# Cross stage of a decoder kernel: rounds of scores placed singly, context in thirds, the FiLM halves of two different tiles in one pass

## The chip, the cores and the metric

The kernel runs on one core of a Trainium2 chip. The metric is the device time of one execution in microseconds (us). The kernel before takes 5044.64 us (median of 3 runs, 5043.18 to 5045.29). PE is the matrix engine (TensorE), ACT the ScalarE, DVE the VectorE, POOL the GpSimd engine, SP the engine that issues most of the DMA transfers. Each engine works through its own queue of instructions in the order in which they are written; semaphores hold an instruction back until another engine has come far enough.

## The reference, cut to what matters

The whole program is one decoder layer on 4 sequences of 1024 tokens, width 512: a causal linear attention, a cross attention with a convolution along the sequence, and a quantised feed-forward network. The change lies in the cross stage, which computes:

```python
scores = einsum('bthd,bghd->bhtg', Q, K) / sqrt(DH)          # 4 heads of 32, 2048 context rows
scores = where(vision_mask, scores, -inf)
topv, topi = top_k(scores, 32)
attn = zeros.at[..., topi].set(softmax(topv))                  # 32 weights a row, zeros elsewhere
attn_mean = attn.mean(axis=1)                                  # mean over the 4 heads
c_t = einsum('btg,bgd->btd', attn_mean, x_vision @ Wv)
scale_in, shift_in = split(c_t @ W_film_in + b_film_in)        # "FiLM", inner half
x = layernorm(x_text) * (1 + gate * scale_in) + gate * shift_in
y = s4d(x, ...)                                                # a long convolution along the sequence
scale_out, shift_out = split(c_t @ W_film_out + b_film_out)    # FiLM, outer half
y = y * (1 + gate * scale_out) + gate * shift_out
```

## The kernel before, in words

The 4096 tokens are 32 tiles of 128 (`TILES`); tile t has 4 heads, and head h of tile t is job j = 4t + h (`NH2` = 4). For every job the cross stage does this:

- **Scores** (PE, `scores`, L1161). For a pair p of heads there are four rounds c, one for each 512 columns of the 2048 context rows. In a round each of the two heads has one product of 32 rows of the array (L1169) and a product of one row that adds the mask (L1170). The two heads use the two banks of the PSUM tile `c_p_s`, and the next round waits until ACT has copied the bank out (`copy_s`, L1334).
- **Scan** (DVE, L1490 to L1498). The 32 largest scores of each row are found by four MAX8 over 2048 columns with three MATCH_REPLACE8 between them. `z_done` tells that the scan of a job is over. Before the third MAX8 of job j stands `invert(j - 1)`, the reciprocal L1483, which needs the sum that ACT forms for job j-1.
- **below** (ACT, L1340 to L1346): after `z_done` the threshold, the amount by which each score lies below it, and the sum of the exponentials. **cut** (POOL, L1555) subtracts that amount times a large factor; **weigh** (ACT, L1352) takes the exponential of the whole row; **diagonal** (ACT, L1358) makes the diagonal matrix of 1/sum.
- **attn** (PE, L1179): 16 products of 128x128 that transpose and scale the weights and add them over the heads in `c_p_a`. After the fourth head ACT copies the sum (`copy_a`, L1363).
- **context** (PE, L1231): 48 products of 128x128, the weights times the context values, into `c_p_m`; ACT copies it (`copy_u`, L1368).
- **film** (PE, L1249 and L1250): two halves, each of 6 products of 128x512 and 2 for the bias. Part 0 is the inner half (copied by `copy_fi`, used by POOL's `modulate`), part 1 the outer half (`copy_fo`, stored by `store_mod`).
- **queries** (PE, L1154 and L1158): the tile's x turned, copied by ACT, and multiplied by Wq.

Into the same queues go the pieces of the convolution, one job of 64 channels in a tile of time. `spectra` (PE, L1199: 16 products of 128x64) is copied by `copy_f` (ACT, L1388); POOL then does `transform` (L827 to L850), `convolved` (L1601 to L864) and `finished` (L872 and on), and `slot` (PE, L1219: 16 products of 128x64) makes the output, copied by `copy_slot` (ACT, L1398). For tiles 1 to 8 the jobs are those of the convolution's own kernel, which have no `convolved` and whose `slot` is eight short transposes; from tile 10 on the spectra, and from tile 11 on the slots too, are those of the data.

All of it is one order written by hand for each engine: the loop over t in the blocks of PE (L1255), ACT (L1403), POOL and SP. `c_p_m` has two banks and is shared by the turned x, the queries, spectra, context, slot and film, so the waits in these functions (for `fo_copied`, `q_copied`, `f_copied`, `slot_copied`, `uT_copied`) say who had to be copied out before. The ring `c_s` has five rows: the scores of pair 1 of a tile need attn of job 4t-2 done, those of pair 0 of the next tile attn of job 4t.

## Time and profile before

| | us |
|---|---|
| median of the runs | 5044.64 |
| the profiled execution | 5042.79 |
| its span, first to last instruction | 5040.9 |
| the scans of DVE in the cross stage, first to last | 978.34 to 3378.4 |
| PE busy | 4416.3 (88%) |
| DVE busy | 3805.5 (75%) |
| ACT busy | 2068.8 (41%) |
| POOL busy | 2186.9 (43%) |

The profiled execution is 1.9 us below the median. The span is cut into 40 slices of 126 us; slices 8 to 27 are the cross stage. Times below are from the span's start. "L1179" is line 1179 of the kernel before. In the line of an operation the name ahead of the arrow is what it writes, and those behind it are what it reads. A bracket at the end of a line gives the time that the engine sat idle just before, and who ended it. "issue" there means that the profile shows no other engine as the one that was waited for.

### The profile page before, as it was taken

How to read it: one execution, taken by the hardware profiler on the slowest of the kernel's cores; microseconds unless marked ns; L12 is line 12 of the kernel's file. 1: busy time of each engine (PE TensorE's matmuls, PEld its weight loads, DVE VectorE, ACT ScalarE, POOL GpSimd, SP SyncE). 2: the span in 40 equal slices, each digit the busy share in tenths (PEclk: the TensorE clock that was granted, in tenths of full speed). 3: DMA queues.
4: the chain of work that ended last, by engine and by line, in shares of the span. 5: the costliest groups of instructions: out<-in, count | busy, mean ns of one | idle time of the engine just before them, and what ended most of it. 6: DMA issues, size and time to landing. Idle time of an engine off the chain costs nothing. (4 is left out here: it accounts for less than half of the span.)

```text
span 5040.9 us, 70529 instructions
## 1 busy us (share of the span) xinstructions
PE 4416.3 (88%) x28066; PEld 3194.9 (63%) x28066; DVE 3805.5 (75%) x4097; ACT 2068.8 (41%) x3816; POOL 2186.9 (43%) x2260
## 2 busy tenths in 40 slices
PE   8999977589999999999999999987579989898984
PEld 6777753356665676676766667667456666666662
DVE  5666659699999988888788887876256767777667
ACT  3433322144444444444444444431234545444453
POOL 1111116435454566766667666670233333333321
PEclk9999988678888877777777777788789999999996
DMA  2111115300011001111011110023531211111101
GB/s 84 51 46 50 49 48 185 118 24 28 24 42 61 26 28 34 38 53 36 28 32 38 54 37 26 30 69 76 193 104 43 61 44 58 47 58 54 51 26 36
DMA packets 214587, 275.98 MB, mean 55 GB/s; under 512 B 96659, under 2 KB 144403, under 8 KB 210224
## 3 DMA queue, kind: packets, MB, share of 16 engines
q1 hardware_dynamic: 196850, 216.91, 14.2%
q0 software_dynamic: 17408, 54.56, 2.9%
q8 instruction: 222, 3.64, 0.3%
q14 instruction: 107, 0.88, 0.1%
HBM read 186.44 MB, written 84.98 MB: 54 GB/s over the span
## 5 line engine op out<-in xcount | busy, mean ns | idle before, releaser
L1555 POOL TENSOR_TENSOR c_s<-c_s,c_z 128x2048 f32<-128x2048 f32 x128 | 580.5, 4535 | 792.8 <-ACT c_z L1344 790.8
L1875 PE MATMUL f_p_g<-f_hT,f_w 128*128 128x128 f32 x4096 | 538.3, 295 | 69.8 <-ACT f_gT L1975 55.4
L1496 DVE MAX8 c_top<-c_z 128x8 f32<-128x2048 f32 x256 | 585.0, 2285 | 4.7 <-issue 0.2
L1875 PEld LDWEIGHTS f_p_g<-f_hT,f_w 128*128 128x128 f32 x4096 | 526.7, 211 | 90.4 <-ACT f_gT L1975 58.2
L1497 DVE MATCH_REPLACE8 c_z<-c_top,c_z 128x2048 f32<-128x2048 f32 x256 | 582.6, 2276 | 0.0
L1169 PE MATMUL c_p_s<-c_kt,c_qT 32*128 32x512 f32 x1024 | 500.9, 864 | 87.1 <-ACT c_s L1334 85.8
L1179 PEld LDWEIGHTS c_p_a<-c_diag,c_s 128*128 128x128 f32 x4096 | 528.2, 211 | 49.5 <-ACT c_diag L1358 25.8
L1179 PE MATMUL c_p_a<-c_diag,c_s 128*128 128x128 f32 x4096 | 531.3, 293 | 25.2 <-ACT c_diag L1358 25.2
L1883 PE MATMUL f_p_o<-f_w,f_gT 128*128 128x512 f32 x1024 | 481.8, 592 | 0.0
L1334 ACT ACTIVATE c_s<-c_p_s 128x512 f32<-128x512 f32 x512 | 278.2, 594 | 455.0 <-PE c_p_s L1170 454.6
L1249 PE MATMUL c_p_m<-c_wf,c_uT 128*128 128x512 f32 x768 | 415.7, 684 | 22.6 <-ACT c_yb L1398 16.3
L1231 PE MATMUL c_p_m<-c_aT,c_vals 128*128 128x128 f32 x3072 | 393.3, 296 | 38.1 <-ACT c_fz L1388 33.4
L1231 PEld LDWEIGHTS c_p_m<-c_aT,c_vals 128*128 128x128 f32 x3072 | 387.3, 211 | 42.5 <-ACT c_fz L1388 37.5
L1169 PEld LDWEIGHTS c_p_s<-c_kt,c_qT 32*128 32x128 f32 x1024 | 173.7, 233 | 294.7 <-ACT c_s L1334 283.9
L1249 PEld LDWEIGHTS c_p_m<-c_wf,c_uT 128*128 128x128 f32 x768 | 164.4, 222 | 213.8 <-issue 211.7
L1498 DVE MAX8 c_top<-c_z 128x8 f32<-128x2048 f32 x128 | 293.8, 2295 | 4.4
L1490 DVE MAX8 c_top<-c_s 128x8 f32<-128x2048 f32 x128 | 293.8, 2295 | 4.4
L1491 DVE MATCH_REPLACE8 c_z<-c_top,c_s 128x2048 f32<-128x2048 f32 x128 | 291.3, 2276 | 0.0
L2124 DVE TENSOR_TENSOR f_hs<-f_p_c,f_rs 128x257 f32<-128x257 f32 (+1 forms) x256 | 108.6, 424 | 232.1 <-PE f_p_c L1894 230.6
L1352 ACT ACTIVATE c_s<-c_s,c_nb 128x2048 f32<-128x2048 f32 x128 | 255.2, 1994 | 27.9 <-POOL c_s L1555 27.9
L1344 ACT ACTIVATE c_z<-c_s,c_tb 128x2048 f32<-128x2048 f32 x128 | 256.3, 2002 | 0.0
L1883 PEld LDWEIGHTS f_p_o<-f_w,f_gT 128*128 128x128 f32 x1024 | 174.5, 190 | 123.8 <-issue 115.8
(362 smaller groups left out, 8103.4 us busy)
## 6 DMA issues: line engine op xcount, KB each, us to landing
mod_out<-c_fo POOLq DMA_DIRECT2D x32, 512.0 KB, 3.0
f_mr<-mod_out SPq DMA_DIRECT2D x32, 512.0 KB, 4.8
p_ct<-in_ctxT SPq DMA_DIRECT2D x16, 768.0 KB, 5.1
c_vals<-in_ctx SPq DMA_DIRECT2D x4, 3072.0 KB, 12.0
c_kb<-kspec SPq DMA_DIRECT2D x22, 512.0 KB, 3.3
a_xt<-in_xT SPq DMA_DIRECT2D x32, 256.0 KB, 3.1
a_xr<-in_x SPq DMA_DIRECT2D x32, 256.0 KB, 2.6
x<-a_out POOLq DMA_DIRECT2D x32, 256.0 KB, 2.5
```

The costliest lines, as they stand in the source:

```text
L1169: mm(p_s[:, i, :], qT[r:r + HS, t % 2, :], kt[r:r + HS, cols], start=True, stop=False)
L1179: last = mm(p_a[:, n, :], s[:, j % RING, n * P:(n + 1) * P], diag[:, j % 2, :], start=(h == 0 and n % 4 == 0), stop=(h == NH2 - 1 and n % ...
L1231: last = mm(p_m[:, 0, k * P:(k + 1) * P], vals[:, n, k * P:(k + 1) * P], aT[:, n, :], start=(k == 0 and n == 0), stop=(k == KV3 - 1 and n ...
L1249: mm(p_m[:, n, :], uT[:, k, :], wf[:, k, c * D:(c + 1) * D], start=(k == 0), stop=False)
L1490: st.link(v.max(best[0], row))
L1491: st.link(v.match_replace(work, best[0], row, NEG))
L1496: st.link(v.max(best[n], work))
L1497: st.link(v.match_replace(work, best[n], work, NEG))
L1498: v.max(best[3], work).then_inc(z_done, 1)
L1555: pool.tensor_tensor(row, row, low, ALU.subtract).then_inc(cut_ready, 1)
L1875: last = mm(p_g[:, f % 8, :], w1[:, k, f * P:(f + 1) * P], hT[:, k * P:(k + 1) * P], start=(k == 0 and f % 4 == 0), stop=(k == KD - 1 and ...
L1883: last = mm(p_o[:], gT[:, f, :], w2[:, f, :], start=(f == 0), stop=(f == FT - 1))
```

## The change

`queries(t)` is split in `turn(t)` and `queries(t)`, `scores(t, p)` becomes four calls of `scores(t, p, c)`, and `context(t)` three calls of `context(t, k)` with 16 products each. On PE a round of scores now stands alone between other work; the inner half of FiLM for tile t-1 stands at the end of iteration t, and the outer half of tile t-2 in its first part (before, both halves of tile t-1 stood in iteration t). ACT's copies follow: `copy_q` is split in `copy_x` and `copy_q`, `copy_s` copies one round (2 pieces) at a time instead of two (4 pieces), `copy_f` stands behind weigh and diagonal of job 4t instead of ahead of them, `copy_slot` behind the weigh of job 4t+2 instead of ahead of `below` of it, and `copy_u` behind the copies of two rounds. On POOL `modulate(t - 2)` stands behind `cut(j - 1)` where `modulate(t - 1)` stood behind `cut(j + 2)`, and `store_mod(t - 2)` behind `cut(j)`. SP's queue and DVE's queue are unchanged, and no instruction's shape changes.

```diff
--- before.py
+++ after.py
@@ -1147,27 +1147,28 @@
             pe.wait_ge(core_in, 16 * 3)
             pe.wait_ge(consts, 2)
 
-            def queries(t):
+            def turn(t):
                 pe.wait_ge(x_in[t % 2], 16 * (t // 2 + 1))
                 at_least(pe, fo_copied, t - 2)
                 for k in range(KD):
                     last = nc.tensor.transpose(p_m[:, 0, k * P:(k + 1) * P], xt[:, k * P:(k + 1) * P], ident[:])
                 last.then_inc(xT_done, 1)
+
+            def queries(t):
                 pe.wait_ge(xT_copied, t + 1)
                 for k in range(KD):
                     last = mm(p_m[:, 1, 0:P], wq[:, k, :], xT[:, k * P:(k + 1) * P], start=(k == 0), stop=(k == KD - 1))
                 last.then_inc(q_done, 1)
 
-            def scores(t, p):
+            def scores(t, p, c):
                 pe.wait_ge(q_copied, t + 1)
                 pe.wait_ge(keys_in, 80 * (t // CH + 1))
-                for c in range(4):
-                    cols = slice(c * 512, (c + 1) * 512)
-                    for i in range(2):
-                        r = HS * (2 * p + i)
-                        at_least(pe, s_copied, (t * 2 + p) * 8 + 2 * c + i - 1)
-                        mm(p_s[:, i, :], qT[r:r + HS, t % 2, :], kt[r:r + HS, cols], start=True, stop=False)
-                        mm(p_s[:, i, :], oneb[r:r + 1, :], mrow[r:r + 1, cols], start=False, stop=True).then_inc(s_done, 1)
+                cols = slice(c * 512, (c + 1) * 512)
+                for i in range(2):
+                    r = HS * (2 * p + i)
+                    at_least(pe, s_copied, (t * 2 + p) * 8 + 2 * c + i - 1)
+                    mm(p_s[:, i, :], qT[r:r + HS, t % 2, :], kt[r:r + HS, cols], start=True, stop=False)
+                    mm(p_s[:, i, :], oneb[r:r + 1, :], mrow[r:r + 1, cols], start=False, stop=True).then_inc(s_done, 1)
 
             def attn(j):
                 t, h = j // NH2, j % NH2
@@ -1220,18 +1221,19 @@
                                       start=(n == 0 and r == 0), stop=(n == RX - 1 and r == 1), skip_group_check=True)
                 last.then_inc(slot_done, 1)
 
-            def context(t):
-                at_least(pe, f_copied, forwards(t + 1))
-                pe.wait_ge(values_in, 16 * (t // CH + 1))
-                pe.wait_ge(aT_copied, t + 1)
-                if t + 2 < TILES:
-                    pe.wait_ge(xT_copied, t + 3)
-                for k in range(KV3):
-                    for n in range(GB):
-                        last = mm(p_m[:, 0, k * P:(k + 1) * P], vals[:, n, k * P:(k + 1) * P], aT[:, n, :],
-                                  start=(k == 0 and n == 0), stop=(k == KV3 - 1 and n == GB - 1),
-                                  skip_group_check=True)
-                last.then_inc(uT_done, 1)
+            def context(t, k):
+                if k == 0:
+                    at_least(pe, f_copied, forwards(t + 1))
+                    pe.wait_ge(values_in, 16 * (t // CH + 1))
+                    pe.wait_ge(aT_copied, t + 1)
+                    if t + 2 < TILES:
+                        pe.wait_ge(xT_copied, t + 3)
+                for n in range(GB):
+                    last = mm(p_m[:, 0, k * P:(k + 1) * P], vals[:, n, k * P:(k + 1) * P], aT[:, n, :],
+                              start=(k == 0 and n == 0), stop=(k == KV3 - 1 and n == GB - 1),
+                              skip_group_check=True)
+                if k == KV3 - 1:
+                    last.then_inc(uT_done, 1)
 
             def film(t, part):
                 if part == 0:
@@ -1250,35 +1252,58 @@
                     last = mm(p_m[:, n, :], oneb[0:BR, :], fb[:, c * D:(c + 1) * D], start=False, stop=True)
                 last.then_inc(fo_done if part else fi_done, 1)
 
+            turn(0)
             queries(0)
-            scores(0, 0)
+            for c in range(4):
+                scores(0, 0, c)
             for t in range(TILES):
                 j = t * NH2
+
                 if t:
                     attn(j - 2)
-                scores(t, 1)
+                scores(t, 1, 0)
+                if t > 1:
+                    film(t - 2, 1)
+                scores(t, 1, 1)
+                if t + 1 < TILES:
+                    turn(t + 1)
+
+                if t:
+                    attn(j - 1)
+                scores(t, 1, 2)
                 if t + 1 < TILES:
                     queries(t + 1)
-                if t:
-                    attn(j - 1)
                 if forward_job(t) is not None:
                     spectra(t)
+                scores(t, 1, 3)
                 if t:
-                    context(t - 1)
+                    context(t - 1, 0)
+
                 attn(j)
                 if t + 1 < TILES:
-                    scores(t + 1, 0)
+                    scores(t + 1, 0, 0)
+                if t:
+                    context(t - 1, 1)
+                if t + 1 < TILES:
+                    scores(t + 1, 0, 1)
+                if t:
+                    context(t - 1, 2)
+
+                attn(j + 1)
+                if t + 1 < TILES:
+                    scores(t + 1, 0, 2)
                 if slot_job(t) is not None:
                     slot(t)
+                if t + 1 < TILES:
+                    scores(t + 1, 0, 3)
                 if t:
                     film(t - 1, 0)
-                attn(j + 1)
-                if t:
-                    film(t - 1, 1)
             attn(LAST - 1)
+            film(TILES - 2, 1)
             attn(LAST)
             slot(TILES)
-            context(TILES - 1)
+            for k in range(KV3):
+                context(TILES - 1, k)
             film(TILES - 1, 0)
 
             def rest_forward(i):
@@ -1319,19 +1344,20 @@
         def _(act):
             a = nc.scalar.activation
 
-            def copy_q(t):
+            def copy_x(t):
                 act.wait_ge(xT_done, t + 1)
                 at_least(act, q_done, t)
                 a(xT[:], p_m[:, 0, :], ACT.Copy).then_inc(xT_copied, 1)
+
+            def copy_q(t):
                 act.wait_ge(q_done, t + 1)
                 a(qT[:, t % 2, :], p_m[:, 1, 0:P], ACT.Copy).then_inc(q_copied, 1)
 
-            def copy_s(t, p, part):
+            def copy_s(t, p, c):
                 at_least(act, attn_done, (t - 1) * NH2 + 2 * p + 1)
-                for c in range(2 * part, 2 * part + 2):
-                    for i in range(2):
-                        act.wait_ge(s_done, (t * 2 + p) * 8 + 2 * c + i + 1)
-                        a(s[:, (t * NH2 + 2 * p + i) % RING, c * 512:(c + 1) * 512], p_s[:, i, :], ACT.Copy).then_inc(s_copied, 1)
+                for i in range(2):
+                    act.wait_ge(s_done, (t * 2 + p) * 8 + 2 * c + i + 1)
+                    a(s[:, (t * NH2 + 2 * p + i) % RING, c * 512:(c + 1) * 512], p_s[:, i, :], ACT.Copy).then_inc(s_copied, 1)
 
             def below(j):
 
@@ -1397,49 +1423,60 @@
                     at_least(act, y_out, 16 * (g - NCB))
                     a(yb[:].rearrange("p n c -> p (n c)"), p_m[:, 1, :], ACT.Copy).then_inc(slot_copied, 1)
 
+            copy_x(0)
             copy_q(0)
-            copy_s(0, 0, 0)
-            copy_s(0, 0, 1)
+            for c in range(4):
+                copy_s(0, 0, c)
             for t in range(TILES):
                 j = t * NH2
+
                 if t:
                     below(j - 1)
                 if t > 1:
-                    copy_fo(t - 2)
+                    copy_fi(t - 2)
                 copy_s(t, 1, 0)
                 if t:
                     weigh(j - 1)
                     diagonal(j - 1)
+                if t > 1:
+                    copy_fo(t - 2)
                 copy_s(t, 1, 1)
                 if t + 1 < TILES:
-                    copy_q(t + 1)
+                    copy_x(t + 1)
 
                 below(j)
                 if t:
                     copy_a(t - 1)
+                copy_s(t, 1, 2)
+                if t + 1 < TILES:
+                    copy_q(t + 1)
+                weigh(j)
+                diagonal(j)
                 if forward_job(t) is not None:
                     copy_f(t)
-                weigh(j)
-                diagonal(j)
+                copy_s(t, 1, 3)
 
                 below(j + 1)
-                if t:
-                    copy_u(t - 1)
                 if t + 1 < TILES:
                     copy_s(t + 1, 0, 0)
                 weigh(j + 1)
                 diagonal(j + 1)
                 if t + 1 < TILES:
                     copy_s(t + 1, 0, 1)
+                if t:
+                    copy_u(t - 1)
+
+                below(j + 2)
+                if t + 1 < TILES:
+                    copy_s(t + 1, 0, 2)
+                weigh(j + 2)
                 if slot_job(t) is not None:
                     copy_slot(t)
-
-                below(j + 2)
-                if t:
-                    copy_fi(t - 1)
-                weigh(j + 2)
                 diagonal(j + 2)
+                if t + 1 < TILES:
+                    copy_s(t + 1, 0, 3)
             below(LAST)
+            copy_fi(TILES - 2)
             weigh(LAST)
             diagonal(LAST)
             copy_fo(TILES - 2)
@@ -1621,21 +1658,22 @@
                 if t:
                     cut(j - 1)
                 if t > 1:
+                    modulate(t - 2)
+                cut(j)
+                if t > 1:
                     store_mod(t - 2)
-                cut(j)
                 if job is not None:
                     transform(t)
                 cut(j + 1)
                 if job is not None and not of_kernel(job):
                     convolved(t)
                 cut(j + 2)
-                if t:
-                    modulate(t - 1)
                 if job is not None and not of_kernel(job):
                     finished(t)
                 if t < NCB:
                     skip(t)
             cut(LAST)
+            modulate(TILES - 2)
             store_mod(TILES - 2)
             modulate(TILES - 1)
             store_mod(TILES - 1)
```

The first place is PE, from the context of a tile to the inner half of FiLM (`c_p_a<-c_diag,c_s` is attn, `c_p_s` the scores, `c_fv` the slot, `c_wf` the FiLM). Before:

```order
L1231 MATMUL c_p_m<-c_aT,c_vals 128x128 x48
L1179 MATMUL c_p_a<-c_diag,c_s 128x128 x16
L1169 MATMUL c_p_s<-c_kt,c_qT 128x512
L1170 MATMUL c_p_s<-c_mrow,c_oneb 128x512
...
L1219 MATMUL c_p_m<-c_fv,c_gm 128x64 x16
L1249 MATMUL c_p_m<-c_wf,c_uT 128x512 x3
L1250 MATMUL c_p_m<-c_fb,c_oneb 128x512
```

The two rows of the scores stand eight times in a row there, which is four rounds of two heads. Now ("..." stands for the rest of a round, and for a whole round where it follows a row of another kind):

```order
L1232 MATMUL c_p_m<-c_aT,c_vals 128x128 x16
L1180 MATMUL c_p_a<-c_diag,c_s 128x128 x16
L1170 MATMUL c_p_s<-c_kt,c_qT 128x512
L1171 MATMUL c_p_s<-c_mrow,c_oneb 128x512
...
L1232 MATMUL c_p_m<-c_aT,c_vals 128x128 x16
...
L1232 MATMUL c_p_m<-c_aT,c_vals 128x128 x16
L1180 MATMUL c_p_a<-c_diag,c_s 128x128 x16
...
L1220 MATMUL c_p_m<-c_fv,c_gm 128x64 x16
...
L1251 MATMUL c_p_m<-c_wf,c_uT 128x512 x3
L1252 MATMUL c_p_m<-c_fb,c_oneb 128x512
```

The four rounds of the pair moved apart: one behind attn of head 0, one between the second and third part of the context, one behind attn of head 1, one behind the slot.

The second place is ACT, around the copy of the slot (`c_yb`; `c_z<-c_s,c_tb` is the amount of `below`, `c_topx,c_den` its sum, `c_s<-c_s,c_nb` weigh, `c_s<-c_p_s` copies of scores, `c_fi` the copy of the inner half). Before:

```order
L1352 ACTIVATE c_s<-c_s,c_nb 128x2048
L1358 ACTIVATE c_diag<-c_identm,c_rd 128x128
L1334 ACTIVATE c_s<-c_p_s 128x512 x4
L1398 ACTIVATE c_yb<-c_p_m 128x512
L1340 ACTIVATE c_tb<-c_top 128x1
L1341 ACTIVATE c_nb<-c_top 128x1
L1344 ACTIVATE c_z<-c_s,c_tb 128x2048
L1346 ACTIVATE c_topx,c_den<-c_top,c_nb 128x32
L1373 ACTIVATE c_fi<-c_p_m 128x1024
```

Now:

```order
L1366 ACTIVATE c_tb<-c_top 128x1
L1367 ACTIVATE c_nb<-c_top 128x1
L1370 ACTIVATE c_z<-c_s,c_tb 128x2048
L1372 ACTIVATE c_topx,c_den<-c_top,c_nb 128x32
L1360 ACTIVATE c_s<-c_p_s 128x512 x2
L1378 ACTIVATE c_s<-c_s,c_nb 128x2048
L1424 ACTIVATE c_yb<-c_p_m 128x512
L1384 ACTIVATE c_diag<-c_identm,c_rd 128x128
L1360 ACTIVATE c_s<-c_p_s 128x512 x2
L1366 ACTIVATE c_tb<-c_top 128x1
L1367 ACTIVATE c_nb<-c_top 128x1
...
L1399 ACTIVATE c_fi<-c_p_m 128x1024
```

The copy of the slot moved from ahead of `below` of job 4t+2 to behind the weigh of that job, the last round of scores for the next tile stands behind it, and only then comes `below` of job 4t+3 and the copy of the inner half.

## Rows read from the trace of the kernel before

**Rows 1.** The page, part 2: PE's granted clock in tenths, 40 slices.

```profile
PEclk9999988678888877777777777788789999999996
```

**Rows 2.** Timeline of DVE, first MAX8 of jobs: start us, us, operation.

```profile
978.34 2.29 DVE L1490 MAX8 c_top<-c_s 128x8 f32<-128x2048 f32 x1
1744.70 2.29 DVE L1490 MAX8 c_top<-c_s 128x8 f32<-128x2048 f32 x1
...
2012.39 2.29 DVE L1490 MAX8 c_top<-c_s 128x8 f32<-128x2048 f32 x1
2028.93 2.29 DVE L1490 MAX8 c_top<-c_s 128x8 f32<-128x2048 f32 x1
...
3312.24 2.29 DVE L1490 MAX8 c_top<-c_s 128x8 f32<-128x2048 f32 x1
```

**Rows 3.** Waits from 1400 to 3650 us: total, times, longest.

```profile
DVE c_rd L1483 <- issue: 262.8, 47, 10.6
```

**Rows 4.** Timeline of ACT and DVE in tile 14.

```profile
2038.23 1.08 ACT L1334 ACTIVATE c_s<-c_p_s 128x512 f32<-128x512 f32 x2 [2.10 <-PE c_p_s L1170]
2045.74 0.60 ACT L1398 ACTIVATE c_yb<-c_p_m 128x512 f32<-128x512 f32 x1 [6.42 <-PE c_p_m L1219]
2048.85 0.16 DVE L1483 RECIPROCAL c_rd<-c_den 128x1 f32<-128x1 f32 x1 [10.52 <-issue]
```

**Rows 5.** Timeline of PE: attn, scores, slot, FiLM, attn, scores.

```profile
2028.44 1.13 PE L1169 MATMUL c_p_s<-c_kt,c_qT 32*128 32x512 f32 x4
2038.61 1.76 PE L1219 MATMUL c_p_m<-c_fv,c_gm 128*128 128x64 f32 x7
2046.48 4.66 PE L1249 MATMUL c_p_m<-c_wf,c_uT 128*128 128x512 f32 x6 [0.78 <-ACT c_yb L1398]
2053.99 3.73 PE L1179 MATMUL c_p_a<-c_diag,c_s 128*128 128x128 f32 x32
2057.56 2.74 PE L1249 MATMUL c_p_m<-c_wf,c_uT 128*128 128x512 f32 x6
2063.15 3.73 PE L1179 MATMUL c_p_a<-c_diag,c_s 128*128 128x128 f32 x32
2066.82 1.13 PE L1169 MATMUL c_p_s<-c_kt,c_qT 32*128 32x512 f32 x4
2067.78 0.39 PE L1170 MATMUL c_p_s<-c_mrow,c_oneb 1*128 1x512 bf16 x2
```

**Rows 6.** Windows: us, busy time of the engines, PE's granted clock, DMA.

```profile
2026.30:2029.70 3.40, 3.40 (x26) 2.42 (x25) 3.33 (x3) 0.00 (x0) 3.40 (x2) 1.00 0.02 5
2033.20:2050.20 17.00, 15.99 (x49) 10.27 (x47) 6.41 (x6) 7.04 (x12) 9.66 (x11) 0.50 0.15 46
2070.70:2084.30 13.60, 12.46 (x42) 8.68 (x42) 11.57 (x9) 8.30 (x15) 0.81 (x1) 0.50 0.44 155
```

**Rows 7.** Timeline, one convolution job: spectra, copies, and POOL.

```profile
2007.53 3.68 PE L1199 MATMUL c_p_m<-c_cx,c_fm 128*128 128x64 f32 x32
2007.73 1.88 ACT L1363 ACTIVATE c_aT<-c_p_a 128x2048 f32<-128x2048 f32 x1 [2.53 <-PE c_p_a L1179]
2011.25 1.02 ACT L1388 ACTIVATE c_fz<-c_p_m 128x1024 f32<-128x1024 f32 x1 [1.64 <-PE c_p_m L1199]
2012.35 1.28 POOL L827 TENSOR_TENSOR c_fw<-c_fz 128x512 f32<-128x512 f32 x1 [2.83 <-ACT c_fz L1388]
2024.00 4.54 POOL L1555 TENSOR_TENSOR c_s<-c_s,c_z 128x2048 f32<-128x2048 f32 x1
2028.49 2.35 POOL L1601 TENSOR_TENSOR c_fz<-c_fw,c_kb 128x1024 f32<-128x1024 f32 x1
2032.88 1.99 ACT L1352 ACTIVATE c_s<-c_s,c_nb 128x2048 f32<-128x2048 f32 x1
2040.80 0.73 POOL L864 TENSOR_TENSOR c_ft<-c_fz 128x256 f32<-128x256 f32 x1
```

**Rows 8.** Timeline of ACT, end of the stage: the last copy of `c_aT`.

```profile
3403.75 1.87 ACT L1363 ACTIVATE c_aT<-c_p_a 128x2048 f32<-128x2048 f32 x1
```

## The prediction

> **What bounds the kernel now.** I began with the page's row of TensorE's granted clock: nine tenths at both ends of the span, seven or eight in the cross stage, slices 8 to 27 [rows 1]. The timeline of DVE gives the pace of that stage. A job that waits for nothing takes 2028.93 - 2012.39 = 16.54 us, so a tile of four can't take under 66.2. From the first scan to that of tile 11 it took 766.4 us, 69.7 a tile, and from there to tile 31 1567.5 us, 78.4 a tile [rows 2]. So DVE, though it does most of the work, waits 12.3 us in each of the later 20 tiles and 3.5 in each of the first 11. The view of waits puts nearly all of it on the reciprocal: 262.8 us in 47 waits, the longest 10.6 [rows 3]. Its operand is the sum that ACT forms in `below`. ACT sat idle 6.42 us for the slot's products just before, with `below` queued behind, and DVE stood 10.52 [rows 4]. So the reader should look at PE: between attn and the slot are the four rounds of scores, from 2028.44 to 2038.61, 10.2 us [rows 5]. At full clock one round, four products of 32 rows and their masks, lasts 1.35 us (2066.82 to 2068.17) [rows 5]; the rest is the ping-pong with ACT's copies (1.08 a round [rows 4]) and the clock. That was 1.00 to 2029.7, then 0.50 (1.2 GHz) from 2033.2 to 2050.2 and again from 2070.7 to 2084.3, each time 4 to 5 us after rounds of scores had begun at 2028.44 and 2066.82 [rows 5, 6]. The slot falls in the slow stretch, 7.1 us (2038.61 to 2045.7) [rows 4, 5]; so do half of the inner FiLM half (7.5 us from 2046.48 to 2053.99, against 5.6 from 2057.56 to 2063.15) and attn of another job [rows 5, 6]. About 31 of 78.5 us are slow. PE binds here with waits in it: at full clock its work is four attn of 3.66 (2063.15 to 2066.82), context 3 x 3.66, eight rounds of 1.35, spectra and slot of 3.68 each, two FiLM halves of 5.6, queries some 1.9 (half an attn), 56.9 us in all [rows 5, 7].
>
> The Trainium skill, "TensorE: Matmul & The Clock Gate", Part 1, says that the gate follows how busy the engine has lately been. This trace does not bear out "busy" as the profile counts it: from 2033.2 to 2050.2 PE is busy 15.99 of 17 us at half clock [rows 6]. By the page's rule alone the scores would not be to blame and to place them singly would give back no clock; only long gaps would count.
>
> **The change part by part.** No work is added: the same products and copies, only in another order. Four things happen.
>
> *Rounds stand singly.* No stretch of scores is longer than 1.35 us at full clock, and the 128x128 or 128x512 work around each is 3.66 or 5.6. The copy of a round (1.08) lies beside that work, so the ping-pong is gone. The row nearest to such a mixture is 2026.3 to 2029.7: two thirds attn, one third scores, and the clock stayed 1.00 in it and after it [rows 5, 6]. I take it that these mixtures hold the clock. This removes PE as the bound: 56.9 is under 66.2.
>
> *The convolution moves back on ACT.* `copy_f` now stands behind weigh and diagonal of job 4t, and `copy_slot` behind the weigh of job 4t+2, whose cut stands on POOL behind `convolved`. This makes a new ring, and it is what I expect to set the pace once PE doesn't. From one `copy_slot` to the next, with durations at full clock:
> - copy_slot 0.60 [rows 4]; inner FiLM half 5.59, attn 3.66, a round 1.35, outer half 5.59, a round 1.35, turning x 0.94 (a quarter of an attn, as four of its products), attn 3.66 [rows 5]: 22.7;
> - `copy_a` 1.88 behind it, the copies of a round 1.08, the queries' copy 0.3 (half of the 0.60 for 512 columns): 26.0. Only then may spectra start, 3.68, and `copy_f`, 1.02 [rows 4, 7]: 30.7;
> - POOL: transform 11.65 (2012.35 to 2024.00), cut 4.49 (to 2028.49), convolved 13.04 (to 2041.53), cut 4.49 [rows 7]: 64.4;
> - weigh 2.0 [rows 7]: 66.4. Seven handovers of 0.1 (2012.27 to 2012.35 is one [rows 7]): 67.1.
> So the ring is 0.9 over DVE's own 66.2 even when nothing in it is slow.
>
> *A gap on PE.* In that ring PE has done its rounds and the slot long before `copy_slot` lets FiLM start. Counted from the start of a scan of job 4t: attn of job 4t+1 starts at about 50, round, slot and round end at 60, and the FiLM half starts at 67. A gap of 7 us costs the clock I think, and then the half takes 7.5 as it did at 2046.48 instead of 5.6 [rows 5]: +1.9. The page's rule agrees here with the price, and by it alone the tile would be 67.1 + 1.9 = 69.0.
>
> *Spectra.* Ahead of it are a round, the queries (0.94) and a wait of some 1 us for the queries' copy; behind it another round. If products of 64 columns count as little as scores, that is a stretch of over 8 us without full work, longer than the 4 to 5 that were enough before [rows 5, 6]. The bounds are 0 and +3.4 (slot at half clock 7.1 against 3.68 [rows 4, 5, 7]); I take the middle, +1.6, since the fall would come after spectra has begun. Below nothing it can't go: spectra ran at full clock before [rows 6, 7].
>
> So a tile from 11 on takes 67.1 + 1.9 + 1.6 = 70.6 us, with bounds 67.1 and 74 (a FiLM half at half clock throughout is 11.2, but the clock came back during it before). In tiles 1 to 10 there is no `convolved`: the cut of job 4t+2 isn't held, the ring is 13 shorter, and DVE's 66.2 decides, even with both surcharges.
>
> *Edits at nothing.* The last round of a pair now stands directly ahead of the `below` behind which DVE needs it, where a whole job lay between. In my walk it is copied 1 us before DVE asks; if it is later, that is the ring's wait seen from DVE and counted already. `modulate` one iteration later: its store feeds convolution loads first needed a tile on; SP's `load_xn` waits for it with a tile's slack. The keys of the next sequence (3 times) are asked for behind the last round, at about 31, for use at 38; where that is short it costs a us or two, three times, inside the range. What is queued behind ACT's wait for the cut of 4t+2 is `copy_slot`, diagonal, the last round and `below`; PE and DVE both wait for these, which is why the ring shows on DVE. The end: the last context began 93.5 us after the last tile's first scan (3403.75 + 1.87 against 3312.24 [rows 2, 8]); by the same walk it begins at 94 to 97 now: +2.
>
> Sum: 11 tiles, 729 against 766.4, -37; 20 tiles, 1412 against 1567.5, -155; end +2. Together -190 on the profiled 5042.8, that is 4853; the median of the runs is 1.9 higher, and I forecast 4854.
>
> **Rivals.**
> - *The ring at full clock* (tile 67.1 to 68.5). For it: 128x128 work on both sides of everything. Against: the gap of 7 us. -(1567.5 - 1342) - 37 = -262, 4782; up to 4812.
> - *More of PE goes slow* (72.5 to 78.4 a tile): a full-clock stretch isn't kept through rounds and the 64-column products, so attn, rounds and the outer half in the ring pay too. For it: two falls in each tile of before [rows 6], and a ring in which 26 us are PE's. 4892 to 5010.
> - *Slower*: if single rounds do not count as full work, their dilution keeps the clock at 0.50 through the tile. PE's 56.9 then tends to 114. The point from which it decides: 56.9 plus half the slow time exceeds 78.5, so over 43 slow us in a tile (31 now). All slow would be 35 us a tile for 20 tiles and 40 for 11, about 6190; just over the point some 5060 to 5200. Against: 2026.3 to 2029.7 at 1.00 [rows 6].
> - *It does nothing*: the wait on the reciprocal only moves to the start of the scans at the same 78.5. The ring would need 8 us that I don't see. About 5040.
>
> **How the numbers follow.** Forecast with a tile of 68.5 to 72.5 (4812 to 4892): 0.45. Ring at full clock: 0.20. More slow: 0.27. Slower: 0.05. Nothing: 0.03. The range 4785 to 4965 leaves out the very fastest ends, the upper third of the third case, and the last two. A measurement tells 0.2%, 10 us, from no change. Faster 0.93, same 0.02, slower 0.05.
>
> **What would show it.** Right: starts of tiles' scans 66.2 apart up to tile 11 and near 70.6 after it; no waits over 1 us at the reciprocal, 3 to 5 us instead ahead of the first MAX8 of a tile, released by ACT's copy of scores; the copy of the slot idle for nothing but weigh's wait for POOL; PE idle 6 to 8 us ahead of the inner half, and that half over 7 us; the granted clock near 1.00 through attn, rounds and context. Wrong: a clock of 0.50 behind single rounds, waits that stay at the reciprocal, or a spacing over 74.

## The result and the profile after

The changed kernel takes 4805.07 us (median of 4 runs, 4799.81 to 4812.83), the kernel before 5044.97 in the same runs. The ratio is 0.9526, with a 95% interval of 0.951 to 0.9543: 240 us less. The profiled execution took 4804.69 us, its span 4802.7. The lines of the changed kernel have other numbers: L1527 is the first MAX8 of a job (L1490 before), L1251 the FiLM (L1249), L1180 attn, L1200 spectra, L1220 the slot, L1370 the amount of `below`, L1378 weigh, L1424 the copy of the slot, L1354 the copy of the queries, L1360 copies of scores, L1592 the cut.

First the page's row of PE's granted clock, which answers to [rows 1]:

```profile
PEclk9999997758889889999999999987999999999996
```

It is five to nine in the cross stage's first part, tiles 0 to 10 (0.84 on average, where it was 0.80); behind it (0.92, where it was 0.78), where the tiles have convolution work, it is nearly as high as elsewhere. The timeline of DVE gives the pace, as [rows 2] did (start us, us, operation, idle before it):

```profile
984.48 2.29 DVE L1527 MAX8 c_top<-c_s 128x8 f32<-128x2048 f32 x1 [0.91 <-ACT c_s L1360]
1713.72 2.29 DVE L1527 MAX8 c_top<-c_s 128x8 f32<-128x2048 f32 x1 [1.43 <-ACT c_s L1360]
...
3079.40 2.29 DVE L1527 MAX8 c_top<-c_s 128x8 f32<-128x2048 f32 x1 [2.15 <-ACT c_s L1360]
```

From tile 0 to tile 11 it is 729.2 us, 66.3 a tile, and from there to tile 31 1365.7 us, 68.3 a tile: 37.1 and 201.9 less than before. The start of the stage is 6.1 us later; later stages and the end of this one are 5.2 us shorter together. The waits say where DVE stands now (total, times, longest; the stretch 1400 to 3350 us):

```profile
DVE c_top L1527 <- ACT c_s L1360: 44.3, 21, 2.9
```

The 262.8 us at the reciprocal [rows 3] are gone. What is left is 2.1 us ahead of the scan of each tile's first job, released by ACT's copy of a round. The tile whose scans begin at 2464.98 (tile 22) shows why. First PE:

```profile
2475.82 0.39 PE L1171 MATMUL c_p_s<-c_mrow,c_oneb 1*128 1x512 bf16 x2
2476.14 2.84 PE L1251 MATMUL c_p_m<-c_wf,c_uT 128*128 128x512 f32 x6
...
2490.64 3.76 PE L1200 MATMUL c_p_m<-c_cx,c_fm 128*128 128x64 f32 x32 [0.84 <-ACT c_qT L1354]
...
2523.87 0.39 PE L1171 MATMUL c_p_s<-c_mrow,c_oneb 1*128 1x512 bf16 x2
2532.08 4.55 PE L1251 MATMUL c_p_m<-c_wf,c_uT 128*128 128x512 f32 x6 [7.82 <-ACT c_yb L1424]
2536.69 2.74 PE L1251 MATMUL c_p_m<-c_wf,c_uT 128*128 128x512 f32 x6
2539.48 3.73 PE L1180 MATMUL c_p_a<-c_diag,c_s 128*128 128x128 f32 x32
```

PE has nothing to do for 7.82 us until the slot is copied. The inner FiLM half then takes 7.40 us (2532.08 to 2539.48), the answer to 7.51 and 5.59 in [rows 5]. Spectra takes 3.76, full speed. ACT and POOL in the same tile:

```profile
2494.43 1.02 ACT L1414 ACTIVATE c_fz<-c_p_m 128x1024 f32<-128x1024 f32 x1 [0.43 <-PE c_p_m L1200]
2495.55 1.27 POOL L827 TENSOR_TENSOR c_fw<-c_fz 128x512 f32<-128x512 f32 x1 [3.36 <-ACT c_fz L1414]
2507.24 4.53 POOL L1592 TENSOR_TENSOR c_s<-c_s,c_z 128x2048 f32<-128x2048 f32 x1
2511.73 2.37 POOL L1638 TENSOR_TENSOR c_fz<-c_fw,c_kb 128x1024 f32<-128x1024 f32 x1
2524.90 4.52 POOL L1592 TENSOR_TENSOR c_s<-c_s,c_z 128x2048 f32<-128x2048 f32 x1
2529.45 2.00 ACT L1378 ACTIVATE c_s<-c_s,c_nb 128x2048 f32<-128x2048 f32 x1 [9.01 <-POOL c_s L1592]
2531.36 0.58 ACT L1424 ACTIVATE c_yb<-c_p_m 128x512 f32<-128x512 f32 x1
```

POOL works without a pause from 2495.55 to the end of the second cut; ACT waits 9.01 us for it, with the slot's copy, the last round and `below` behind. That is the ring of the prediction: copy of the slot, FiLM half, attn, outer half, attn, spectra, POOL, weigh, and again the copy of the slot. The windows, as [rows 6] (us, busy times, granted clock before the last two numbers):

```profile
2467.50:2525.00 57.50, 54.88 (x372) 41.18 (x371) 56.68 (x39) 27.54 (x42) 41.36 (x43) 1.00 0.12 37
2525.50:2535.50 10.00, 3.42 (x4) 1.51 (x5) 7.76 (x5) 6.05 (x10) 9.84 (x17) 0.50 0.10 26
```

Full clock through 57.5 us with all eight rounds in them, and half clock only in the gap and the first 3.5 us behind it: 10 slow us of 68.3. Before it was 34 of 78.5; the prediction's 31 left out a third fall, of 3.4 us, behind spectra and a wait of 1.11:

```profile
2012.70:2016.10 3.40, 3.40 (x18) 3.40 (x18) 3.37 (x3) 3.40 (x5) 3.32 (x5) 0.51 0.00 0
```

In tiles 1 to 8, where the slot is eight short transposes, single rounds don't always hold the clock. In tile 5 a round, the transposes and the next round stand in a row, and the clock goes to 0.50 in the second round, before PE has to wait (PE, then the window):

```profile
1365.08 1.13 PE L1170 MATMUL c_p_s<-c_kt,c_qT 32*128 32x512 f32 x4
1366.36 1.09 PE L1215 MATMUL c_p_m<-c_ident,c_kb 64*128 64x64 f32 x8
1368.08 2.46 PE L1170 MATMUL c_p_s<-c_kt,c_qT 32*128 32x512 f32 x4 [0.62 <-ACT c_s L1360]
```

```profile
1368.50:1370.50 2.00, 2.00 (x6) 0.71 (x4) 1.97 (x2) 0.00 (x0) 2.00 (x1) 0.50 0.84 258
```

It costs nothing there, since DVE's 66.2 us are longer.

### The profile page after: what moved, and what is told of

Its sections match the earlier page's. It is cut to its first block and busy times, and to the rows that moved or that the text cites. A ratio compares the mean times of both kernels' runs of the same rounds, so it can differ in the third digit from the quotient of the medians.

```text
span 4802.7 us, 70845 instructions
## 1 busy us (share of the span) xinstructions
PE 4064.0 (85%) x28066; PEld 2950.6 (61%) x28066; DVE 3799.6 (79%) x4097; ACT 2066.0 (43%) x3816; POOL 2187.5 (46%) x2260
## 5 line engine op out<-in xcount | busy, mean ns | idle before, releaser
L1592 POOL TENSOR_TENSOR c_s<-c_s,c_z 128x2048 f32<-128x2048 f32 x128 | 580.1, 4532 | 549.7 <-ACT c_z L1370 546.3
L1251 PE MATMUL c_p_m<-c_wf,c_uT 128*128 128x512 f32 x768 | 415.0, 683 | 189.1 <-ACT c_yb L1424 165.5
L1180 PE MATMUL c_p_a<-c_diag,c_s 128*128 128x128 f32 x4096 | 491.8, 279 | 40.5 <-ACT c_diag L1384 40.5
L1180 PEld LDWEIGHTS c_p_a<-c_diag,c_s 128*128 128x128 f32 x4096 | 480.4, 195 | 62.0 <-ACT c_diag L1384 50.2
L1378 ACT ACTIVATE c_s<-c_s,c_nb 128x2048 f32<-128x2048 f32 x128 | 256.4, 2003 | 448.4 <-POOL c_s L1592 448.3
L1251 PEld LDWEIGHTS c_p_m<-c_wf,c_uT 128*128 128x128 f32 x768 | 162.4, 220 | 411.5 <-issue 406.1
L1232 PEld LDWEIGHTS c_p_m<-c_aT,c_vals 128*128 128x128 f32 x3072 | 369.6, 201 | 67.9 <-issue 51.1
L1360 ACT ACTIVATE c_s<-c_p_s 128x512 f32<-128x512 f32 x512 | 276.1, 591 | 305.6 <-PE c_p_s L1171 305.6
L1170 PE MATMUL c_p_s<-c_kt,c_qT 32*128 32x512 f32 x1024 | 317.3, 681 | 23.0 <-ACT c_s L1360 21.2
L1527 DVE MAX8 c_top<-c_s 128x8 f32<-128x2048 f32 x128 | 293.8, 2295 | 48.9 <-ACT c_s L1360 45.3
L1370 ACT ACTIVATE c_z<-c_s,c_tb 128x2048 f32<-128x2048 f32 x128 | 256.4, 2003 | 0.0
L244 PE MATMUL a_p_z<-a_xt,a_w 128*128 128x128 f32 x2048 | 236.9, 277 | 10.9 <-DMA a_w<-in_W_attn 10.9
```

What stands on the lines that cost most here:

```text
L1170: mm(p_s[:, i, :], qT[r:r + HS, t % 2, :], kt[r:r + HS, cols], start=True, stop=False)
L1180: last = mm(p_a[:, n, :], s[:, j % RING, n * P:(n + 1) * P], diag[:, j % 2, :], start=(h == 0 and n % 4 == 0), stop=(h == NH2 - 1 and n % ...
L1232: last = mm(p_m[:, 0, k * P:(k + 1) * P], vals[:, n, k * P:(k + 1) * P], aT[:, n, :], start=(k == 0 and n == 0), stop=(k == KV3 - 1 and n ...
L1251: mm(p_m[:, n, :], uT[:, k, :], wf[:, k, c * D:(c + 1) * D], start=(k == 0), stop=False)
L1527: st.link(v.max(best[0], row))
L1592: pool.tensor_tensor(row, row, low, ALU.subtract).then_inc(cut_ready, 1)
```

## The experiments

All were compared with the kernel before on their chip; ratios are given with their 95% intervals. Ahead of each stands its edit, or a sentence that tells it. No run takes the context in thirds, the moved outer half or ACT's and POOL's new order alone, so the share of each in the 240 us isn't measured.

### What made the clock fall: rows of the array

**b_full_rows**, the kernel before with one operand changed:

```diff
-mm(p_s[:, i, :], qT[r:r + HS, t % 2, :], kt[r:r + HS, cols], start=True, stop=False)
+mm(p_s[:, i, :], qT[:, t % 2, :], kt[:, cols], start=True, stop=False)
```

> The kernel before in its own order; only the scores products take all 128 rows of the array instead of 32 (so all four heads are summed in each score; no longer the reference's scores, and the top-32 choice is over other numbers). Columns, counts, waits and copies stay. Theory A (the rows that a product fills decide the clock): the stretches at 1.2 GHz behind the scores go, the slot and the inner FiLM half run at full rate, a tile from 11 on takes 66 to 70 us instead of 78.5, in all 4790 to 4880 us. Rival B (the clock follows busy time, or the ping-pong with ACT's copies is what costs): same busy time, same ping-pong, clock 0.50 in the same places, 5030 to 5050 us.

Measured: 4896.07 us, ratio 0.9686 (0.9662 to 0.9709), 71.7 us a tile from 11 on. The direction is A's, the size not, and the trace says why: a product of 128 rows takes PE 1.37 us for each head, 2.75 a round, where two heads of 32 rows take 1.35 together. Products on different rows of the array had been running side by side, and the edit took that away: 11 us more PE work in a tile, and still 7 us less time. So it needed a fairer partner:

**b_two64**, 64 rows for each head, rows 0 to 63 and 64 to 127:

```diff
-r = HS * (2 * p + i)
+r = 64 * i
-mm(p_s[:, i, :], qT[r:r + HS, t % 2, :], kt[r:r + HS, cols], start=True, stop=False)
+mm(p_s[:, i, :], qT[r:r + 64, t % 2, :], kt[r:r + 64, cols], start=True, stop=False)
```

> The kernel before in its own order; the two heads' products of a round take 64 rows each (0 to 63 and 64 to 127) instead of 32 each, so that together they fill the array and still overlap (each score sums two heads; no longer the reference's scores). In b_full_rows a round of 128-row products took 2.75 us instead of 1.35, since they can't overlap, which hid the clock's share. Theory A (the rows filled decide the clock; a round stays 1.35): clock near 1.00, PE's work 56.9 us a tile plus some 10 of waits, a tile 66 to 68 us from 11 on, 4755 to 4820 us. Rival B (only more columns streamed keep the clock, not rows): clock falls as before, 5030 to 5050 us.

Measured: 5429.79 us, ratio 1.0740 (1.0701 to 1.0778), some 90 us a tile. A was wrong in its premise: 64-row products don't overlap either, a head takes 1.37 us as with 128 rows. That makes the two kernels the clean pair that I had missed: the same products in the same order with the same durations at full clock, and only the rows differ. PE in four rounds, and the windows of them, first with 64 rows:

```profile
2034.38 1.12 PE L1169 MATMUL c_p_s<-c_kt,c_qT 64*128 64x512 f32 x2
2035.44 0.39 PE L1170 MATMUL c_p_s<-c_mrow,c_oneb 1*128 1x512 bf16 x1
2035.75 1.12 PE L1169 MATMUL c_p_s<-c_kt,c_qT 64*128 64x512 f32 x2
...
2040.38 2.07 PE L1169 MATMUL c_p_s<-c_kt,c_qT 64*128 64x512 f32 x2
```

```profile
2034.40:2039.00 4.60, 4.60 (x11) 1.43 (x11) 4.53 (x4) 1.59 (x3) 4.60 (x3) 1.00 0.00 0
2039.50:2063.00 23.50, 22.72 (x52) 11.39 (x52) 6.88 (x5) 8.08 (x13) 10.28 (x11) 0.50 0.11 33
```

Then with 128 rows, a whole stretch of four rounds:

```profile
2538.01 1.12 PE L1169 MATMUL c_p_s<-c_kt,c_qT 128*128 128x512 f32 x2
2539.07 0.38 PE L1170 MATMUL c_p_s<-c_mrow,c_oneb 1*128 1x512 bf16 x1
2539.39 1.12 PE L1169 MATMUL c_p_s<-c_kt,c_qT 128*128 128x512 f32 x2
```

```profile
2536.70:2548.30 11.60, 10.99 (x26) 3.05 (x26) 11.43 (x9) 6.13 (x9) 3.68 (x2) 1.00 0.11 45
```

With 64 rows PE is 22.72 of 23.5 us busy and the clock is at half; with 128 rows it is busy 10.99 of 11.6 and the clock stays. Over tiles 11 to 30 the granted clock is 0.75 with 64 rows and 0.99 with 128. Busy time doesn't decide, filled rows do. It costs 5430 - 4896 = 534 us here.

**a_full_rows** and **a_two64** are the same edits in the changed kernel.

> The changed kernel with the scores products over all 128 rows of the array (all four heads summed in each score; no longer the reference's scores). Theory A (placed singly, the 32-row rounds cost no clock any more; what is left of slow clock comes from the gap alone): same time, 4798 to 4812 us, and the FiLM half behind the gap still takes 7.4. Rival B (single 32-row rounds still cost clock somewhere in the ring): faster by more than 10 us.

> The changed kernel with the same 64-row products. Theory A (32-row rounds placed singly already hold the clock; the gap ahead of the FiLM half is left): a round stays 1.35 us, a tile 68.3, 4798 to 4812 us. Rival B (32-row rounds cost clock even singly): faster by over 10 us.

Measured: 4871.02 us (0.9654, 0.9638 to 0.9671) and 4957.48 us (0.9805, 0.9770 to 0.9840). The times of neither expectation hold, since both rested on a round of 1.35 us; with rounds of 2.75 a tile takes 71.6 and 70 to 75 us. The FiLM half behind the gap does take 7.36 in a_full_rows, as expected, though the gap is only 2.58 there. On single 32-row rounds they say nothing clean; the 57.5 us at 1.00 in the trace after do. But the two are a second clean pair: with the rounds single, 64 rows against 128 cost 4957 - 4871 = 86 us, where they cost 534 in fours, at 0.93 against 0.98 of the clock over tiles 11 to 30. So single rounds take most of the price away, and not all of it.

### Was PE the bound before, or the order of ACT's queue?

**b_slot_late**, the kernel before with the slot's copy moved:

```diff
-                if slot_job(t) is not None:
-                    copy_slot(t)
                 below(j + 2)
+                if slot_job(t) is not None:
+                    copy_slot(t)
```

> The kernel before with one line moved on ACT: the slot's copy stands behind below of job 4t+2 instead of ahead of it, so that DVE gets its sum without waiting for the slot. Theory A (PE with its slow stretches bounds the tile, 4.9 us idle of 78.5): the 10.5 us wait of DVE at the reciprocal goes from there and comes back elsewhere; 5000 to 5045 us, nearer to the upper end. Rival B (the order of ACT's queue bounds it, PE has room): DVE starts about 7 us earlier in each tile from 11 on, 20 x 7 = 140, about 4900 us.

Measured: 5068.77 us, ratio 1.0039 (1.0024 to 1.0054). Tiles from 12 on take 78.5 us as before, and DVE waits at the reciprocal for 273.7 us in 68 waits, the longest 7.7, instead of 262.8 us in 47 waits, the longest 10.6 (both in the stretch 1400 to 3350 us): the wait only moved. Tiles 2 to 8 take 74.7 us instead of 71.1 on average, 25 us together, and tile 11 takes 7 less; that makes it slower than A's 5000 to 5045 too. B is out. The wait that the profile shows on DVE was not the bound. That PE was is borne out by b_full_rows, which changes nothing but PE's products and moves the tile by 6.7 us.

### Singly or together

**a_fours0**, the changed kernel with pair 0's four rounds together, where PE runs ahead of the others:

```diff
-scores(t + 1, 0, 0); context(t - 1, 1); scores(t + 1, 0, 1); context(t - 1, 2)
-attn(j + 1); scores(t + 1, 0, 2); slot(t); scores(t + 1, 0, 3)
+for c in range(4): scores(t + 1, 0, c)
+context(t - 1, 1); context(t - 1, 2); attn(j + 1); slot(t)
```

(conditions left out; ACT's four `copy_s` stand together ahead of weigh of job 4t+1.)

> The changed kernel with the four rounds of pair 0 together again, behind attn of job 4t (on ACT their copies together ahead of the weigh of job 4t+1); they lie in the part of the tile in which PE runs ahead and then waits 7.8 us. Theory A (what PE loses there is taken from the gap): the clock falls behind the rounds, some 4 to 6 us are lost, the gap shrinks to 2 to 4 us and may no longer cost the FiLM half its clock: 66.5 to 68.3 a tile, 4765 to 4812 us. Rival B (every stretch of four rounds costs time, wherever it stands): 71 to 73 a tile, 4860 to 4900 us.

**a_fours1** does the same to pair 1, behind attn of job 4t-2, with its copies ahead of weigh of job 4t-1.

> The changed kernel with the four rounds of pair 1 together again, behind attn of job 4t-2, where PE is in the ring that sets the tile. Theory A: between attn and spectra the ring gets 2.7 us longer by the ping-pong and 2 to 3 us by the slow stretch behind it, so 73 to 76 us a tile from 11 on, 4900 to 4960 us; in tiles 1 to 10 nothing or little, since the ring has 13 us to spare there. Rival B (single rounds don't matter, the gain is from ACT's and POOL's order): 4800 to 4815 us.

Measured: a_fours0 4889.63 us (0.9671, 0.9638 to 0.9705), 70.5 a tile from 11 on; a_fours1 5094.45 us (1.0085, 1.0061 to 1.0108), 79.5 a tile. The first fell to B's time, but not for B's reason. Its trace, PE and ACT:

```profile
2420.14 1.13 PE L1170 MATMUL c_p_s<-c_kt,c_qT 32*128 32x512 f32 x4
...
2430.91 10.30 PE L1232 MATMUL c_p_m<-c_aT,c_vals 128*128 128x128 f32 x64
```

```profile
2441.25 0.49 ACT L1388 ACTIVATE c_uT<-c_p_m 128x384 f32<-128x384 f32 x1 [7.45 <-PE c_p_m L1232]
2448.57 2.00 ACT L1372 ACTIVATE c_s<-c_s,c_nb 128x2048 f32<-128x2048 f32 x1 [4.40 <-POOL c_s L1581]
```

The four rounds take 10.8 us, the clock is 0.50 from 2423.5 to 2437, and two thirds of the context 10.3 us instead of 7.7. PE's gap did shrink, from 7.8 to 2.9, as A said. But it still costs the clock: the FiLM half behind it takes 7.1 to 8.7 us. And the copy of the context (`c_uT`) waits on ACT for PE with `below` of job 4t+2 behind it, so the cut starts 2.1 us after POOL is ready for it (2444.01) and the ring grew by another path. I had counted PE's slack and not who else waits for PE there. Of the 85 us, 33 lie in tiles 0 to 10 (69.3 a tile instead of 66.3), which the expectation didn't speak of; they weren't followed. In a_fours1 the rounds take 10.5 us, the FiLM half behind them 7.6, spectra 5.1, and the gap and its price stay: 11 us a tile, against 5 to 8 expected. Tiles 0 to 10 take 71.4 instead of 66.3, against nothing or little expected, so A's 4900 to 4960 is missed as well as B's. With this pair together the whole gain is lost.

### The ring, and opening it

**a_slot_first**, the changed kernel with one line moved on ACT:

```diff
-                weigh(j + 2)
                 if slot_job(t) is not None:
                     copy_slot(t)
+                weigh(j + 2)
```

> The changed kernel with one line moved on ACT: the slot's copy stands ahead of the weigh of job 4t+2, not behind it. Theory A (the ring through POOL's convolution, weigh and the slot's copy sets 68.3 us a tile; the 7.8 us gap on PE ahead of the FiLM half comes from it): the ring is open, the gap and its slow clock go, DVE's 66.2 a tile decides; 20 x 2.1 = 42 less, 4755 to 4770 us. Rival B (68.3 is set by PE's work and the clock, the gap is only what is left over): no change, 4800 to 4810 us, and the gap stands elsewhere.

Measured: 4783.70 us, ratio 0.9473 (0.9458 to 0.9487), 67.5 a tile: half of what A gave. The gap ahead of the FiLM half is gone, and another has come:

```profile
2474.30 7.06 PE L1200 MATMUL c_p_m<-c_cx,c_fm 128*128 128x64 f32 x32 [4.35 <-ACT c_qT L1354]
...
2513.51 2.84 PE L1251 MATMUL c_p_m<-c_wf,c_uT 128*128 128x512 f32 x6
```

PE is so early now that spectra waits for the queries' copy, which waits on ACT for the scan; the clock is 0.50 from 2472 to 2489 and spectra takes 7.06. So this kernel is 21 us faster with more slow clock in a tile, some 15 us on average instead of 10. I take the new ring to be one scan, the copies, this slow spectra and POOL's chain.

**a_q_first** moves the queries' copy alone; **a_both** makes both moves:

```diff
+                if t + 1 < TILES:
+                    copy_q(t + 1)
                 if t:
                     copy_a(t - 1)
                 copy_s(t, 1, 2)
-                if t + 1 < TILES:
-                    copy_q(t + 1)
```

> The changed kernel with the second of these moves alone: the queries' copy ahead of the copy of the heads' sum and of a round. Theory A (the ring through copy_slot, FiLM half, attn, outer half, attn, spectra and POOL sets 68.3): the queries' products end only 0.4 us ahead of where their copy stands now, so the ring gets 0.4 us shorter, 8 us in all, 4792 to 4803 us. Rival B (the copies of 1.88 and 1.08 us lie in the ring whole, as the prediction summed them): 3 us a tile shorter, so 66.2 a tile, 42 us in all, about 4763 us.

> The changed kernel with two moves on ACT: the slot's copy ahead of the weigh of job 4t+2 (as a_slot_first, 67.5 us a tile), and the queries' copy directly behind below of job 4t, ahead of the copy of the heads' sum and of a round. In a_slot_first PE sat idle 4.4 us ahead of spectra, waiting for the queries' copy, and spectra ran at 1.2 GHz, 7.06 us instead of 3.76. Theory A (the gap is what costs the clock, and spectra at half rate lies in a ring through POOL and one scan): the gap shrinks by 3 us to 1.4, spectra takes 3.76, the ring is 6 us shorter and DVE's 66.2 decides in all tiles: 1.35 x 20 = 27 less than 4783.7, 4750 to 4762 us. Rival B (something else holds the 67.5, as POOL's chain alone): 4775 to 4790 us.

Measured: a_q_first 4813.25 us (0.9541, 0.9527 to 0.9556), which overlaps with the 0.951 to 0.9543 of the changed kernel: no gain that can be told. B is out by 50 us, and A's 8 us didn't come either: its tiles take 68.4 to 70.0 in turns, since the slow stretch around the gap has no fixed length. a_both 4757.16 us (0.9429, 0.9415 to 0.9443), the forecast time, and 66.17 us in every tile: DVE scans without a wait. It is the fastest of all, 48 us under the changed kernel. One part of the expectation was wrong, though: behind a wait of 1.73 spectra takes anything from 3.76 to 7.06 us, 5.8 on average over tiles 12 to 30:

```profile
2461.29 7.06 PE L1200 MATMUL c_p_m<-c_cx,c_fm 128*128 128x64 f32 x32 [1.73 <-ACT c_qT L1354]
2659.80 4.78 PE L1200 MATMUL c_p_m<-c_cx,c_fm 128*128 128x64 f32 x32 [1.73 <-ACT c_qT L1354]
```

The 3 us from the copies' order were enough all the same.

**a_fill** and **a_fill7** put products that nobody reads into the gap instead:

```diff
+                if t > NCB + 2:
+                    pe.wait_ge(uT_copied, t)
+                    for n in range(14):                       # 7 in a_fill7
+                        mm(p_m[:, 0, :], uT[:, n % KV3, :], wf[:, n % KV3, 0:D], start=True, stop=True)
                 if t:
                     film(t - 1, 0)
```

> The changed kernel with 14 products of 128x512 more in each tile from 11 on, placed in PE's gap ahead of the inner FiLM half, written to a bank that the FiLM overwrites; they wait for nothing that is late and last 14 x 0.46 = 6.4 us at full clock in a gap of 7.8. Theory A (the gap costs the clock and the FiLM half then takes 7.4 instead of 5.6, in the ring): faster with more work, a tile 66.5 instead of 68.3, 4765 to 4780 us. Rival B (the FiLM half's slow start isn't in the ring, or the clock doesn't fall for the gap): 4800 to 4810 us; if the filling itself runs slow it ends behind the copy of the slot and the tile gets up to 5 us longer, about 4900 us.

> As a_fill, with 7 products of 128x512 in the gap instead of 14. One such product took 0.91 us at full clock (2.74 us for three), so that 14 lasted 12.3 us and ended 4.3 us behind the copy of the slot; 7 last 6.4 us, up to 8.5 where they start slow, in a gap of 7.8. Theory A (the gap costs the clock and the FiLM half is in the ring): the half takes 5.6, a tile 66.5 to 67.3, 4765 to 4785 us. Rival B: 4800 to 4810 us.

Measured: a_fill 4870.77 us (0.9648, 0.9633 to 0.9662), for a plain error of mine: the row "x6, 2.74 us" is three products of two records each, so one product is 0.91 us and not 0.46. Fourteen last 12.3 us and end 4.3 behind the copy of the slot; PE being in the ring, that shows in the tile (70.6 to 73.5). a_fill7 4781.10 us (0.9479, 0.9460 to 0.9499), 66.5 a tile, with 7 products more per tile than the changed kernel and 24 us faster:

```profile
2372.64 6.28 PE L1302 MATMUL c_p_m<-c_wf,c_uT 128*128 128x512 f32 x14
2380.51 2.81 PE L1251 MATMUL c_p_m<-c_wf,c_uT 128*128 128x512 f32 x6 [1.60 <-ACT c_yb L1428]
```

The FiLM half is back at 5.6 us, and the tile shorter by 1.8, just what the half had lost. This settles both that the gap costs the clock and that the half lies in the ring.

## Why the prediction was right, step by step

- *Rounds stand singly and hold the clock, so PE stops being the bound.* Right for the later tiles: 1.00 for 57.5 us. Among tiles 1 to 8 the clock still falls, in tile 5 at the two rounds around the short transposes, at no cost. b_full_rows against b_two64 shows that it is the rows, and a_fours0 and a_fours1 that rounds of 32 rows in fours lose it.
- *Tiles 0 to 10 at DVE's pace.* 729 forecast, 729.2 measured; -37 and -37.1.
- *The ring through POOL sets the later tiles.* Right in kind: DVE waits ahead of the first scan of a tile, ACT for POOL ahead of the slot's copy, PE in the gap. a_slot_first and a_fill7, which touch nothing else, each move the tile. 70.6 forecast, 68.3 measured, -155.5 against -201.9: 46 of the 49 us by which the forecast was too high are this term.
- *The gap's price*, +1.9: right. Gap 7.82, half 7.40 against 5.59, so +1.8; a_fill7 gives it back.
- *Spectra's price*, +1.6: the step that failed. It was 0: spectra took 3.76 us in every tile from 12 on. The bounds were right and the middle of them was a guess. It makes 32 of the 46 us. The longer the wait ahead of spectra, the more it cost on average, but what sets the price between the bounds isn't shown. Behind 0.84 us it kept the clock in each of these tiles here, and in 31 of 38 tiles of a_fill and a_fill7 (4.6 to 5.1 us in the other 7); behind 3.6 to 4.4 it cost the full 3.3 in every tile of a_slot_first; behind 1.73 it cost 0 to 3.3 in a_both. The tile of 69.0, which the prediction worked out by the rule of the Trainium skill ("TensorE: Matmul & The Clock Gate", Part 1) that the gate follows how busy the engine has lately been, came nearer than 70.6; that it did is no proof of the rule. Counted as the profile counts busy time, b_two64 contradicts it: busy 22.72 of 23.5 us at half clock.
- *The sum of the ring*, 67.1: 66.5 in effect (68.3 less 1.8). Turning x took 0.5 and not 0.94 (2483.20 to 2483.70); the rest is 0.1 each in rounds, handovers and weigh, with the outer half 0.2 longer. The three copies behind attn, 3.26 in the sum, took 3.27 (2487.37 to 2490.64), though moving the queries' one to the front shortens that by only 0.4, since its products end at 2489.80. Small terms, 12 us.
- *Rivals.* The ring at full clock (67.1 to 68.5 a tile, 4782 to 4812) is what the time fell into; it had 0.20, and its tile is right for another reason than it gave, one price of two being there. The 4812 to 4892 that had 0.45 missed it, so it was the width of the range that held the time and not the middle. More slow and Slower didn't come; the mixtures held in the later tiles.
- *The end and the rest*: +2 forecast; the last context began 92.8 us after the last tile's first scan against 93.5, and the later stages and the start changed by -4.5 and +6.1, which the order of this stage doesn't explain: the first scan begins anywhere from 978.34 to 987.20 us in the fourteen traces, and a_fill, the same as the changed kernel up to there, begins it at 978.34 where the changed kernel does at 984.48. Not followed further.

## What to carry to other kernels

The engine that waits longest in the profile is not the one to free: moving the wait alone (b_slot_late) gained nothing, because PE at half clock lay beneath it. Look first at what fills the array's rows in each stretch, keep thin products apart by full ones where the chain runs through PE, and look for gaps in that chain, since a gap costs again what follows it. When one bound goes, write down the next ring at full speed, and then for each gap in it ask who waits there, ACT's queue included.

## What the runs showed of the hardware

- Two products of 32 rows on different rows of the array take 1.35 us together with their masks; two of 64 rows on different halves 2.75, as two of 128. The side-by-side running was there for 32 rows and not for 64.
- At equal busy time, 64-row products lost the clock 4.6 us after they began (2034.4 to 2039) and 128-row products did not in stretches of 11.6.
- The price of a gap didn't grow with its length: the FiLM half took 7.36 us behind a gap of 2.58 (a_full_rows) and 7.40 behind 7.82. Behind 1.60 it took 5.66 (a_fill7), but 7.36 behind 1.73 (a_two64).
- Adding 7 products a tile (a_fill7) made a kernel 24 us faster.
